# The last token group of a LoRA layer: the weighting and the sum of terms on VectorE by halves, the last products by halves, a store for each tile

## The chip, the cores and the metric

The kernel runs on one NeuronCore of one Trainium2 chip. The metric is the device time of one execution in microseconds (us); lower is better. The time before is 794.3 us, the median of three runs (794.25 to 794.47). The engines are named as in the profile: PE is TensorE (PEld its weight loads), DVE is VectorE, ACT is ScalarE, POOL is GpSimd and SP is SyncE, which here only issues transfers.

## What is computed

The reference is two transformer layers over 2048 tokens of width 256: a long convolution in place of attention, a mixture of 16 experts, a second attention, and last a feed-forward layer with LoRA experts. The change lies in that last layer alone:

```
h = layernorm(x);  logits = h @ Wg.T;  the best K = 2 of 8 experts e, with weights rw
for k in 0, 1:                                  # the two picks of each token
    x1 = h @ W1.T + lora(A1[e_k], B1[e_k])      # F = 896 hidden columns, rank 32
    x3 = h @ W3.T + lora(A3[e_k], B3[e_k])
    x2 = silu(x1) * x3
    out += (x2 @ W2.T + lora(A2[e_k], B2[e_k]) of x2) * rw_k
x = x + out
```

## The kernel before

The last phase (`tail_phase`) works on 8 groups of 256 tokens (`NG` = 8 groups of `TG` = 2 tiles of 128). Of each group the 896 hidden columns are taken in 7 chunks of 128 (`FB` = 7), so that there are 56 chunks F. Each engine runs its own program: a loop over steps S in which chunk S is begun and chunks S-1 and S-2 are finished. The order on an engine is the order of the code, and engines wait for each other by semaphores, each counted up by one kind of instruction. No scheduler moves anything.

For chunk F and pick k, PE forms x1 and x3 (`base` L1442, `low_rank` L1457), ACT applies silu (`silu` L1625), and DVE multiplies by x3 (`product` L1953). All of the two picks' output has the factor of the first pick taken out, so the second pick is weighted by the ratio of the two: POOL multiplies it by `ratio_sb` (`weight` L1748) and adds it to the first (`both` L1753). Products of fp32 values are made as three products of a high and a low part, so ACT copies the high parts (`hidden_high` L1631, L1635) and DVE subtracts to get the low parts (`hidden_low` L1959). Then PE multiplies the hidden columns by A2 (`terms` L1489, 6 products of 512 columns, 3 for each half of the 256 expert ranks, in two PSUM banks) and by W2 (`down` L1502, 6 products of 256 columns).

After its 7th chunk a group is closed. DVE multiplies each half of the terms by the picks' masks (`masked_terms` L1969), POOL sums the two picks (`terms_sum` L1764), ACT and DVE form the high and the low part (`terms_high` L1648, `terms_low` L1975), PE multiplies by B2 (`low_rank_out` L1515, 12 products of 256 columns), DVE adds the group to x (`add_out` L1982) and SP stores its two tiles (`store` L1403). In the groups 0 to 6 this happens while the next group's chunks run. Behind group 7 there is no next one: the whole chain lies open. `LAST_CHUNK` is 56.

Of the kernel before, what the change touches and what calls it, by code (L numbers as in the profile page):

```python
# [1283 lines left out]
TG = 2  # L1284
# [31 lines left out]
def tail_phase(nc, memory, a, stage, slots_dram, out_rows, ident, x_sb, comb_idx, norm, w_hi, w_lo, ctx_ring, banks):  # L1316
# [38 lines left out]
    with ExitStack() as s:  # L1355
# [36 lines left out]
        def _(sp):  # L1392
# [8 lines left out]
            def store(g):  # L1401
                sp.wait_ge(out_added, TG * (g + 1))
                sp.dma_start(out_rows[:, TG * g:TG * g + TG, :], x_sb[:, TG * g:TG * g + TG, :]).then_inc(stored, 16)  # L1403

# [6 lines left out]
            for S in range(FIRST_STEP, END_STEP):  # L1411
# [8 lines left out]
                if n == 3 and 1 <= g <= NG:  # L1420
                    store(g - 1)
            sp.wait_ge(stored, 16 * NG)

        @block.tensor
        def _(pe):
# [53 lines left out]
            def terms(F):  # L1479
# [5 lines left out]
                for half in range(HALVES):  # L1485
                    if n == 0 and g >= 1:
                        pe.wait_ge(t_mul, HALVES * (g - 1) + half + 1)
                    for j, (wp, hp) in enumerate(split_products(weight_cols(n, 5, half), hid)):
                        last = nc.tensor.matmul(term_banks[half][:, :], wp, hp, start=(n == 0 and j == 0),  # L1489
                                                stop=(n == FB - 1 and j == 2))  # L1490
                last.then_inc(terms_done, 1)

# [14 lines left out]
            def low_rank_out(g):  # L1507
                pe.wait_ge(t_lo_done, g + 1)
                for t in range(TG):
                    for half in range(HALVES):  # L1510
                        rows = slice(t * P, (t + 1) * P)
                        cols = slice(4 * DIM + half * DIM, 4 * DIM + (half + 1) * DIM)
                        w = w_hi[:, FB, cols], w_lo[:, FB, cols]
                        for k, (hp, wp) in enumerate(split_products((t_hi[:, half, rows], t_lo[:, half, rows]), w)):
                            last = nc.tensor.matmul(out_banks[g % 2][:, t * DIM:(t + 1) * DIM], hp, wp, start=False,  # L1515
                                                    stop=(half == 1 and k == 2), skip_group_check=True)
                last.then_inc(out_done, 1)
# [96 lines left out]
        def _(act):  # L1614
# [12 lines left out]
            def hidden_high(F):  # L1627
                act.wait_ge(weighted, F + 1)
                if F >= 2:
                    act.wait_ge(terms_done, F - 1)  # L1630
                nc.scalar.copy(hid_hi[:, F % 2, SECOND, :], f[:, F % 2, 1, :]).then_inc(hi_done, 1)  # L1631
# [12 lines left out]
            def terms_high(g):  # L1644
                act.wait_ge(t_sum, g + 1)
                if g >= 1:
                    act.wait_ge(out_done, g)
                nc.scalar.copy(t_hi[:, :, :], mix[:, :, 0:GT]).then_inc(t_hi_done, 1)  # L1648

# [72 lines left out]
        def _(pool):  # L1722
# [62 lines left out]
            for S in range(FIRST_STEP, END_STEP):  # L1785
# [5 lines left out]
                if n == 0 and 0 <= g < NG:  # L1791
                    inputs_low(g, 0)
                if n == 2 and 1 <= g <= NG:
                    terms_sum(g - 1)
# [4 lines left out]
                gathers(S)  # L1799
                if is_chunk(S - 1):  # L1800
                    weight(S - 1)
# [5 lines left out]
        def _(dve):  # L1807
# [143 lines left out]
            def product(F, k):  # L1951
                dve.wait_ge(silu_done, 2 * F + k + 1)
                nc.vector.tensor_tensor(f[:, F % 2, k, :], f[:, F % 2, k, :], x_banks[F % 2][:, GT:2 * GT], ALU.mult)\  # L1953
                  .then_inc(prod_done, 1)

            def hidden_low(F):
                for i, which in enumerate((SECOND, BOTH)):
# [4 lines left out]
            def masked_terms(g):  # L1962
                dve.wait_ge(am_lo_pool, 2 * min(g + 2, NG))
                dve.wait_ge(am_lo_dve, 2 * min(g + 2, NG))
                dve.wait_ge(terms_done, FB * (g + 1))
                for half in range(HALVES):
                    by_kind = [v.rearrange("p (w t) -> p w t", w=PICKS) for v in (mix[:, half, :],
                                                                                 term_banks[half][:, :])]
                    nc.vector.tensor_tensor(by_kind[0], by_kind[1],  # L1969
                                            masks_sb[:, g % 2, :, half * GT:(half + 1) * GT], ALU.mult)\  # L1970
                      .then_inc(t_mul, 1)

            def terms_low(g):
                dve.wait_ge(t_hi_done, g + 1)
                nc.vector.tensor_tensor(t_lo[:, :, :], mix[:, :, 0:GT], t_hi[:, :, :].bitcast(FP32), ALU.subtract)\  # L1975
                  .then_inc(t_lo_done, 1)

# [21 lines left out]
            for S in range(FIRST_STEP, END_STEP):  # L1999
# [25 lines left out]
                if is_chunk(S - 1):  # L2025
                    product(S - 1, 1)
                if of_group:
                    inputs_product(g, 3)
# [94 lines left out]
```

## Time and profile before

| | |
|---|---|
| median of 3 runs | 794.3 us (794.25 to 794.47) |
| the profiled execution | 791.16 us, of which the span is 789.4 us |
| mean granted PE clock | 0.959 of full speed |
| busy share of the span | PE 90%, PEld 81%, DVE 64%, POOL 49%, ACT 43% |

The span runs from the first to the last instruction of the profiled execution; 1.76 us of its time lie around it. All times of rows count from the start of the span. "Idle before" in square brackets is how long the engine had nothing to do, and whose work ended that.

### The profile page before, as it was taken

Reading aid. Unit: us, or ns where it says so; the run is one execution under the profiler, and the core shown is the slowest. Engines: PE = TensorE matmul, PEld = TensorE weight load, DVE = VectorE, ACT = ScalarE, POOL = GpSimd, SP = SyncE. Lnnn points to the kernel's source line nnn. Section 1 sums busy time; section 2 is a strip of 40 time slices with the busy share of each in tenths; the row PEclk is TensorE's granted clock in tenths of the full one; section 3 lists DMA queues with packets and bytes.
Section 4 is the critical chain, followed back from the end, with each engine's and each line's share of the span. In section 5 each row is a group of like instructions: output and inputs, shape, how many; then the busy total and the mean of one; then the engine's idle time right before and its main releaser. Section 6 shows DMA issues by size and latency. Waiting matters only on the chain.

```text
span 789.4 us, 13948 instructions
## 1 busy us (share of the span) xinstructions
PE 713.2 (90%) x4849; PEld 635.7 (81%) x4849; DVE 507.8 (64%) x1296; ACT 340.5 (43%) x698; POOL 384.9 (49%) x450
## 2 busy tenths in 40 slices
PE   4899988959999991778999999999999999999995
PEld 2444557848999980668899999999999999999995
DVE  3999997975666645676566566575574675653422
ACT  2563633245666652265444253444434533443221
POOL 5876956047766605544264363543652643322322
PEclk9999998988999995679999999999999999999999
DMA  8675505946866764424021020010020110000000
GB/s 246 196 166 133 142 27 125 210 108 179 245 195 197 163 146 126 155 71 130 1 61 34 8 61 28 14 59 22 29 63 5 41 41 1 2 15 1 14 1 14
DMA packets 44595, 68.61 MB, mean 87 GB/s; under 512 B 7376, under 2 KB 32240, under 8 KB 44528
## 3 DMA queue, kind: packets, MB, share of 16 engines
q0 software_dynamic: 10080, 28.72, 16.5%
q1 hardware_dynamic: 34352, 38.97, 15.5%
q8 instruction: 41, 0.67, 0.4%
q14 instruction: 26, 0.21, 0.1%
q10 hardware_dynamic: 96, 0.04, 0.0%
HBM read 50.77 MB, written 14.84 MB: 83 GB/s over the span
## 4 chain that ended last, share of the span: by engine, by line
PE 53%; POOL 3%; DVE 2%; ACT 2%; issue 2%; POOLq 0%; DVEq 0%
PE psum L1457 20%; PE psum L1442 10%; PE psum L1489 9%; PE psum L1502 4%; PE psum L1475 3%; PE psum L1538 2%; PE psum L1515 2%; PE psum L1528 2%; POOL rows_back L1728 1%; PE psum L1556 1%; ACT lora_w_hi L1618 1%; DVE lora_w_lo L1819 0%; PE psum L1546 0%; PE psum L1569 0%; PE psum L1576 0%
## 5 line engine op out<-in xcount | busy, mean ns | idle before, releaser
L1953 DVE TENSOR_TENSOR hid<-hid,psum 128x256 f32<-128x256 f32 x112 | 47.0, 420 | 152.2 <-ACT hid L1625 152.2
L1457 PE MATMUL psum<-am_hi,lora_w_hi 128*128 128x256 f32 x448 | 127.4, 284 | 2.0 <-DVE am_lo L1948 2.0
L1748 POOL TENSOR_TENSOR hid<-hid,ratio_sb 128x256 f32<-128x256 f32 x56 | 41.5, 741 | 176.9 <-DVE hid L1953 176.7
L1457 PE MATMUL psum<-am_hi,lora_w_lo 128*128 128x256 f32 x448 | 127.4, 284 | 0.0
L1457 PE MATMUL psum<-am_lo,lora_w_hi 128*128 128x256 f32 x448 | 127.2, 284 | 0.0
L1625 ACT ACTIVATE hid<-psum 128x256 f32<-128x256 f32 x112 | 42.9, 384 | 183.3 <-PE psum L1457 183.2
L1033 POOL DMA_INDIRECT rows_in<-y_scratch,slot_token x80 | 76.0, 950 | 30.9 <-issue 26.5
L1457 PEld LDWEIGHTS psum<-am_hi,lora_w_hi 128*128 128x128 f32 x448 | 86.2, 192 | 2.2 <-POOL am_lo L1759 2.1
L1457 PEld LDWEIGHTS psum<-am_hi,lora_w_lo 128*128 128x128 f32 x448 | 86.3, 193 | 0.0
L1457 PEld LDWEIGHTS psum<-am_lo,lora_w_hi 128*128 128x128 f32 x448 | 86.2, 192 | 0.0
L1728 POOL DMA_INDIRECT rows_back<-slots_scratch,comb_idx x64 | 66.8, 1043 | 39.2 <-POOLq L697 23.7
L1442 PE MATMUL psum<-lora_x_hi,lora_w_hi 128*128 128x256 f32 x224 | 67.8, 302 | 3.5 <-DVE lora_w_lo L1819 3.5
L1959 DVE TENSOR_TENSOR hid_lo<-hid,hid_hi 128x256 fp32r<-128x256 f32 x112 | 56.8, 528 | 13.1 <-ACT hid_hi L1631 8.0
L1442 PE MATMUL psum<-lora_x_lo,lora_w_hi 128*128 128x256 f32 x224 | 63.1, 282 | 0.0
L327 POOL TENSOR_TENSOR kv<-ctx_t 128x1024 f32<-128x1024 f32 (+2 forms) x48 | 57.4, 1284 | 11.6 <-PE psum L448 11.6
L1442 PE MATMUL psum<-lora_x_hi,lora_w_lo 128*128 128x256 f32 x224 | 62.9, 281 | 0.0
L873 PE MATMUL psum<-moe_w_hi,moe_xt_hi 128*128 x160 | 49.2, 307 | 0.0
L591 DVE TENSOR_TENSOR prod<-psum,q_t 128x1024 f32<-128x1024 f32 (+1 forms) x64 | 41.2, 685 | 8.4 <-PE psum L448 6.2
L1442 PEld LDWEIGHTS psum<-lora_x_hi,lora_w_hi 128*128 128x128 f32 x224 | 42.7, 191 | 4.6 <-DVE lora_w_lo L1819 4.2
L873 PE MATMUL psum<-moe_w_lo,moe_xt_hi 128*128 x160 | 45.9, 287 | 0.0
L1489 PE MATMUL psum<-hid_hi,lora_w_hi 128*128 128x512 f32 x112 | 44.6, 398 | 1.3 <-DVE hid_lo L1959 1.3
L873 PE MATMUL psum<-moe_w_hi,moe_xt_lo 128*128 x160 | 45.4, 284 | 0.0
(250 smaller groups left out, 2050.2 us busy)
## 6 DMA issues: line engine op xcount, KB each, us to landing
slots_scratch<-y_out SPq DMA_DIRECT2D x40, 256.0 KB, 3.3
stage<-in_moe_weights SPq DMA_DIRECT2D x18, 384.0 KB, 3.8
moe_w_lo<-in_moe_weights POOLq DMA_DIRECT2D x18, 384.0 KB, 7.1
lora_stage_early<-in_lora_weights SPq DMA_DIRECT2D x16, 384.0 KB, 3.5
x_sb<-in_x SPq DMA_DIRECT2D x4, 512.0 KB, 6.3
ctx_t<-in_ctx_t SPq DMA_DIRECT2D x4, 512.0 KB, 7.3
y_scratch<-y SPq DMA_DIRECT2D x8, 256.0 KB, 2.2
x_sb<-shared_out POOLq DMA_DIRECT2D x4, 512.0 KB, 5.3
```

The costliest lines, as they stand in the source:

```text
L327: last = nc.gpsimd.tensor_tensor(kv[:, n % KV_SLOTS, :, first:first + shape[2] * shape[3]].rearrange("p n (i j) -> p n i j", j=shape[3]), ...
L591: last = nc.vector.tensor_tensor(prod[:, :, j, i], y_ji, query[:, :, i].unsqueeze(2).broadcast_to(shape), ALU.mult)
L873: last = nc.tensor.matmul(gu_banks[q % 2][:, k * DIM:(k + 1) * DIM], xp, wp, start=(c == 0 and j == 0), stop=(c == HALVES - 1 and j == 2))
L1033: nc.gpsimd.indirect_dma_start(out=rows_in[:, i % ROW_SLOTS, :], out_offset=None, in_=y_dram[:, :], in_offset=bass.IndirectOffsetOnAxis(ap ...
L1442: nc.tensor.matmul(x_banks[F % 2][:, w * GT:(w + 1) * GT], wp, xp, start=(w == 0 and c == 0 and k == 0), stop=False, skip_group_check=True)
L1457: last = nc.tensor.matmul(x_banks[F % 2][:, w * GT:(w + 1) * GT], wp, ap, start=False, stop=(half == 1 and k == 2), skip_group_check=True)
L1489: last = nc.tensor.matmul(term_banks[half][:, :], wp, hp, start=(n == 0 and j == 0), stop=(n == FB - 1 and j == 2))
L1625: nc.scalar.activation(f[:, F % 2, k, :], x_banks[F % 2][:, 0:GT], ACT.Silu).then_inc(silu_done, 1)
L1728: nc.gpsimd.indirect_dma_start(out=rows_back[:, t % ROW_TILES, k * DIM:(k + 1) * DIM], out_offset=None, in_=slots_dram[:, :], in_offset=ba ...
L1748: nc.gpsimd.tensor_tensor(f[:, F % 2, 1, :], f[:, F % 2, 1, :], ratio_sb[:, F // FB % 2, :], ALU.mult)\
L1953: nc.vector.tensor_tensor(f[:, F % 2, k, :], f[:, F % 2, k, :], x_banks[F % 2][:, GT:2 * GT], ALU.mult)\
L1959: nc.vector.tensor_tensor(hid_lo[:, F % 2, which, :], f[:, F % 2, which, :], hid_hi[:, F % 2, which, :].bitcast(FP32), ALU.subtract).then_ ...
```

## The change

It touches what follows the last chunk of group 7, and the form of a few semaphores elsewhere.

1. The last chunk (F = 55) is weighted and summed by DVE (`weight_last`), no longer by POOL.
2. `terms_done` counts each half of the terms; in group 7 DVE starts on half 0 with the first count, and sums the two picks itself, half by half.
3. High and low parts of group 7's terms are made by halves of 256 columns in place of 512 at once.
4. `low_rank_out` takes the halves of the ranks in its outer loop and the tiles in the inner one (in all groups), and in group 7 waits for each half on its own.
5. Group 7's two tiles are stored by two transfers of 128 KB in place of one of 256 KB, each behind its own addition.

```diff
--- before.py
+++ after.py
@@ -1399,8 +1399,10 @@
                 load_ctx(sp, a, ctx_ring, b, ctx_loaded[b % CTX_SLOTS])
 
             def store(g):
-                sp.wait_ge(out_added, TG * (g + 1))
-                sp.dma_start(out_rows[:, TG * g:TG * g + TG, :], x_sb[:, TG * g:TG * g + TG, :]).then_inc(stored, 16)
+                step = TG if g < NG - 1 else 1
+                for t in range(TG * g, TG * g + TG, step):
+                    sp.wait_ge(out_added, t + step)
+                    sp.dma_start(out_rows[:, t:t + step, :], x_sb[:, t:t + step, :]).then_inc(stored, 16)
 
             sp.dma_start(gate_sb[:, :, :], a["lora_gate"]).then_inc(gate_loaded, 16)
             for t in range(TG):
@@ -1419,7 +1421,7 @@
                             load_context(t + CTX_SLOTS)
                 if n == 3 and 1 <= g <= NG:
                     store(g - 1)
-            sp.wait_ge(stored, 16 * NG)
+            sp.wait_ge(stored, 16 * (NG - 1 + TG))
 
         @block.tensor
         def _(pe):
@@ -1488,7 +1490,7 @@
                     for j, (wp, hp) in enumerate(split_products(weight_cols(n, 5, half), hid)):
                         last = nc.tensor.matmul(term_banks[half][:, :], wp, hp, start=(n == 0 and j == 0),
                                                 stop=(n == FB - 1 and j == 2))
-                last.then_inc(terms_done, 1)
+                    last.then_inc(terms_done, 1)
 
             def down(F):
                 g, n = F // FB, F % FB
@@ -1506,8 +1508,10 @@
 
             def low_rank_out(g):
                 pe.wait_ge(t_lo_done, g + 1)
-                for t in range(TG):
-                    for half in range(HALVES):
+                for half in range(HALVES):
+                    if half == 1 and g == NG - 1:
+                        pe.wait_ge(t_lo_done, NG + 1)
+                    for t in range(TG):
                         rows = slice(t * P, (t + 1) * P)
                         cols = slice(4 * DIM + half * DIM, 4 * DIM + (half + 1) * DIM)
                         w = w_hi[:, FB, cols], w_lo[:, FB, cols]
@@ -1627,7 +1631,7 @@
             def hidden_high(F):
                 act.wait_ge(weighted, F + 1)
                 if F >= 2:
-                    act.wait_ge(terms_done, F - 1)
+                    act.wait_ge(terms_done, HALVES * (F - 1))
                 nc.scalar.copy(hid_hi[:, F % 2, SECOND, :], f[:, F % 2, 1, :]).then_inc(hi_done, 1)
                 act.wait_ge(both_done, F + 1)
                 if F >= 2:
@@ -1642,10 +1646,15 @@
                 nc.scalar.copy(am_hi[:, kind, w, :], mix[:, w, :]).then_inc(am_hi_done, 1)
 
             def terms_high(g):
-                act.wait_ge(t_sum, g + 1)
                 if g >= 1:
                     act.wait_ge(out_done, g)
-                nc.scalar.copy(t_hi[:, :, :], mix[:, :, 0:GT]).then_inc(t_hi_done, 1)
+                if g < NG - 1:
+                    act.wait_ge(t_sum, g + 1)
+                    nc.scalar.copy(t_hi[:, :, :], mix[:, :, 0:GT]).then_inc(t_hi_done, 1)
+                    return
+                for half in range(HALVES):
+                    act.wait_ge(t_sum, g + half + 1)
+                    nc.scalar.copy(t_hi[:, half, :], mix[:, half, 0:GT]).then_inc(t_hi_done, 1)
 
             def exponentials(G):
                 for k in range(TG):
@@ -1790,14 +1799,14 @@
                         attention_rstd(first, first + (1 if G == 0 else TG))
                 if n == 0 and 0 <= g < NG:
                     inputs_low(g, 0)
-                if n == 2 and 1 <= g <= NG:
+                if n == 2 and 1 <= g < NG:
                     terms_sum(g - 1)
                 if n == 2 and G is not None:
                     router_rstd(G)
                 if n == 3 and G is not None:
                     x_low_part(G)
                 gathers(S)
-                if is_chunk(S - 1):
+                if is_chunk(S - 1) and S < LAST_CHUNK:
                     weight(S - 1)
                     both(S - 1)
                 if n == 0 and 0 <= g < NG:
@@ -1953,6 +1962,15 @@
                 nc.vector.tensor_tensor(f[:, F % 2, k, :], f[:, F % 2, k, :], x_banks[F % 2][:, GT:2 * GT], ALU.mult)\
                   .then_inc(prod_done, 1)
 
+            def weight_last(F):
+                dve.wait_ge(ratio_copied, F // FB + 1)
+                dve.wait_ge(prod_done, 2 * F + 2)
+                nc.vector.tensor_tensor(f[:, F % 2, 1, :], f[:, F % 2, 1, :], ratio_sb[:, F // FB % 2, :], ALU.mult)\
+                  .then_inc(weighted, 1)
+                dve.wait_ge(weighted, F + 1)
+                nc.vector.tensor_tensor(f[:, F % 2, 0, :], f[:, F % 2, 0, :], f[:, F % 2, 1, :], ALU.add)\
+                  .then_inc(both_done, 1)
+
             def hidden_low(F):
                 for i, which in enumerate((SECOND, BOTH)):
                     dve.wait_ge(hi_done, 2 * F + i + 1)
@@ -1962,18 +1980,31 @@
             def masked_terms(g):
                 dve.wait_ge(am_lo_pool, 2 * min(g + 2, NG))
                 dve.wait_ge(am_lo_dve, 2 * min(g + 2, NG))
-                dve.wait_ge(terms_done, FB * (g + 1))
+                if g < NG - 1:
+                    dve.wait_ge(terms_done, HALVES * FB * (g + 1))
                 for half in range(HALVES):
+                    if g == NG - 1:
+                        dve.wait_ge(terms_done, HALVES * FB * NG - HALVES + half + 1)
                     by_kind = [v.rearrange("p (w t) -> p w t", w=PICKS) for v in (mix[:, half, :],
                                                                                  term_banks[half][:, :])]
                     nc.vector.tensor_tensor(by_kind[0], by_kind[1],
                                             masks_sb[:, g % 2, :, half * GT:(half + 1) * GT], ALU.mult)\
                       .then_inc(t_mul, 1)
+                    if g == NG - 1:
+                        dve.wait_ge(t_mul, HALVES * g + half + 1)
+                        nc.vector.tensor_tensor(mix[:, half, 0:GT], mix[:, half, 0:GT], mix[:, half, GT:2 * GT], ALU.add)\
+                          .then_inc(t_sum, 1)
 
             def terms_low(g):
-                dve.wait_ge(t_hi_done, g + 1)
-                nc.vector.tensor_tensor(t_lo[:, :, :], mix[:, :, 0:GT], t_hi[:, :, :].bitcast(FP32), ALU.subtract)\
-                  .then_inc(t_lo_done, 1)
+                if g < NG - 1:
+                    dve.wait_ge(t_hi_done, g + 1)
+                    nc.vector.tensor_tensor(t_lo[:, :, :], mix[:, :, 0:GT], t_hi[:, :, :].bitcast(FP32), ALU.subtract)\
+                      .then_inc(t_lo_done, 1)
+                    return
+                for half in range(HALVES):
+                    dve.wait_ge(t_hi_done, g + half + 1)
+                    nc.vector.tensor_tensor(t_lo[:, half, :], mix[:, half, 0:GT], t_hi[:, half, :].bitcast(FP32),
+                                            ALU.subtract).then_inc(t_lo_done, 1)
 
             def add_out(g):
                 dve.wait_ge(out_done, g + 1)
@@ -2024,6 +2055,8 @@
                     router_masks(G)
                 if is_chunk(S - 1):
                     product(S - 1, 1)
+                if S == LAST_CHUNK:
+                    weight_last(S - 1)
                 if of_group:
                     inputs_product(g, 3)
                 if n == 1:
```

On DVE, this is what follows the product of the last chunk, first before and then after. `hid` is the hidden chunk, `mix` holds the masked terms, `t_hi` and `t_lo` their high and low parts, and x_sb the residual stream.

```order
L1953 TENSOR_TENSOR hid<-hid,psum 128x256 [waits silu_done]
L1959 TENSOR_TENSOR hid_lo<-hid,hid_hi 128x256 [waits hi_done] x2
L1969 TENSOR_TENSOR mix<-psum,masks_sb 128x512 [waits terms_done,am_lo_dve,am_lo_pool]
L1969 TENSOR_TENSOR mix<-psum,masks_sb 128x512
L1975 TENSOR_TENSOR t_lo<-mix,t_hi 128x512 [waits t_hi_done]
L1982 SCALAR_TENSOR_TENSOR x_sb<-psum,lora_first_w,x_sb 128x256 [waits first_w_done,out_done]
L1982 SCALAR_TENSOR_TENSOR x_sb<-psum,lora_first_w,x_sb 128x256
```

```order
L1962 TENSOR_TENSOR hid<-hid,psum 128x256 [waits silu_done]
L1968 TENSOR_TENSOR hid<-hid,ratio_sb 128x256 [waits prod_done,ratio_copied]
L1971 TENSOR_TENSOR hid<-hid 128x256 [waits weighted]
L1977 TENSOR_TENSOR hid_lo<-hid,hid_hi 128x256 [waits hi_done] x2
L1990 TENSOR_TENSOR mix<-psum,masks_sb 128x512 [waits terms_done,am_lo_dve,am_lo_pool]
L1995 TENSOR_TENSOR mix<-mix 128x256 [waits t_mul]
L1990 TENSOR_TENSOR mix<-psum,masks_sb 128x512 [waits terms_done]
L1995 TENSOR_TENSOR mix<-mix 128x256 [waits t_mul]
L2006 TENSOR_TENSOR t_lo<-mix,t_hi 128x256 [waits t_hi_done] x2
L2013 SCALAR_TENSOR_TENSOR x_sb<-psum,lora_first_w,x_sb 128x256 [waits first_w_done,out_done]
L2013 SCALAR_TENSOR_TENSOR x_sb<-psum,lora_first_w,x_sb 128x256
```

Two instructions on `hid` stand ahead of the low parts, two sums on `mix` stand between and behind the masked products, and the low part `t_lo` is made in two.

On SP, this is the end of the list of transfers, before and then after. The rows on `ctx_ring` load a tile of the context for the second attention; `x4` and `x3` stand for so many stores in a row.

```order
L1403 DMA out_x<-x_sb 128x2x256 [waits out_added]
L1276 DMA ctx_ring<-in_ctx_keys 128x256 [waits scaled_done]
L1277 DMA ctx_ring<-in_ctx_t 128x2x128
L1403 DMA out_x<-x_sb 128x2x256 [waits out_added] x4
L1355 UNCONDITIONAL_BRANCH [waits stored]
```

```order
L1405 DMA out_x<-x_sb 128x2x256 [waits out_added]
L1276 DMA ctx_ring<-in_ctx_keys 128x256 [waits scaled_done]
L1277 DMA ctx_ring<-in_ctx_t 128x2x128
L1405 DMA out_x<-x_sb 128x2x256 [waits out_added] x3
L1405 DMA out_x<-x_sb 128x256 [waits out_added] x2
L1355 UNCONDITIONAL_BRANCH [waits stored]
```

The last of the four stores of two tiles has become two stores of one tile each.

On POOL, `weight` and `both` of chunk 55 and the last `terms_sum` are gone; its program ends with chunk 54. On PE no product is added or taken away: the last 12 are the same, with their order by halves, and the seventh has a wait of its own for `t_lo`. On ACT the last copy of 512 columns has become two of 256.

## Rows read from the trace of the kernel before

**Rows 1.** The head of the page

```profile
span 789.4 us, 13948 instructions
```

**Rows 2.** Timeline, the last chunk (start us, us, engine, line, operation, out<-in)

```profile
774.24 0.42 DVE L1953 TENSOR_TENSOR hid<-hid,psum 128x256 f32<-128x256 f32 x1 [2.03 <-ACT hid L1625]
...
774.74 0.73 POOL L1748 TENSOR_TENSOR hid<-hid,ratio_sb 128x256 f32<-128x256 f32 x1 [3.43 <-DVE hid L1953]
...
775.56 0.73 POOL L1753 TENSOR_TENSOR hid<-hid 128x256 f32<-128x256 f32 x1
...
776.32 0.40 ACT L1635 CAST hid_hi<-hid 128x256 fp32r<-128x256 f32 x1 [0.40 <-POOL hid L1753]
...
776.75 0.43 DVE L1959 TENSOR_TENSOR hid_lo<-hid,hid_hi 128x256 fp32r<-128x256 f32 x1 [0.19 <-ACT hid_hi L1635]
...
777.24 0.50 PE L1489 MATMUL psum<-hid_hi,lora_w_hi 128*128 128x512 f32 x1 [1.33 <-DVE hid_lo L1959]
```

**Rows 3.** Timeline, the last terms, their masks, sum and parts

```profile
777.80 0.40 PE L1489 MATMUL psum<-hid_hi,lora_w_lo 128*128 128x512 f32 x1
...
778.51 0.39 PE L1489 MATMUL psum<-hid_hi,lora_w_lo 128*128 128x512 f32 x1
...
778.74 0.28 PE L1502 MATMUL psum<-lora_w_hi,hid_hi 128*128 128x256 f32 x1
...
779.04 1.29 DVE L1969 TENSOR_TENSOR mix<-psum,masks_sb 128x512 f32<-128x512 f32 x2 [1.85 <-PE psum L1489]
...
779.33 0.28 PE L1502 MATMUL psum<-lora_w_hi,hid_lo 128*128 128x256 f32 x1
...
780.40 1.26 POOL L1764 TENSOR_TENSOR mix<-mix 128x512 f32<-128x512 f32 x1 [4.12 <-DVE mix L1969]
...
781.70 0.62 ACT L1648 CAST t_hi<-mix 128x512 fp32r<-128x512 f32 x1 [4.97 <-POOL mix L1764]
...
782.35 0.69 DVE L1975 TENSOR_TENSOR t_lo<-mix,t_hi 128x512 fp32r<-128x512 f32 x1 [2.02 <-ACT t_hi L1648]
```

**Rows 4.** Timeline, the last products, addition and store

```profile
783.09 0.58 PE L1515 MATMUL psum<-lora_w_hi,t_hi 128*128 128x256 f32 x1 [3.49 <-DVE t_lo L1975]
...
786.06 0.88 DVE L1982 SCALAR_TENSOR_TENSOR x_sb<-psum,lora_first_w,x_sb 128x256 f32<-128x256 f32 x2 [3.02 <-PE psum L1515]
...
786.96 0.37 SPq L1403 DMA_DIRECT2D out_x<-x_sb  x1
```

**Rows 5.** Windows, granted clock third from the end, around the last products

```profile
782.50:782.75 0.25, 0.00 (x0) 0.00 (x0) 0.25 (x1) 0.00 (x0) 0.00 (x0) 0.81 0.00 0
...
783.25:784.00 0.75, 0.75 (x4) 0.75 (x5) 0.00 (x0) 0.00 (x0) 0.00 (x0) 0.50 0.00 0
```

**Rows 6.** Timeline, the same products and addition in group 0

```profile
419.10 0.39 PE L1515 MATMUL psum<-lora_w_hi,t_hi 128*128 128x256 f32 x1
...
420.82 0.48 DVE L1982 SCALAR_TENSOR_TENSOR x_sb<-psum,lora_first_w,x_sb 128x256 f32<-128x256 f32 x1 [0.47 <-PE psum L1515]
```

**Rows 7.** Timeline, three other starts of PE after a wait

```profile
379.13 0.39 PE L1442 MATMUL psum<-lora_x_hi,lora_w_hi 128*128 128x256 f32 x1 [1.25 <-DVE lora_w_lo L1819]
...
110.51 2.82 PE L461 MATMUL psum<-ident,q_t 128*128 128x128 f32 x12 [2.24 <-DVE q_t L598]
...
122.84 0.63 PE L473 MATMUL psum<-ident,y 128*128 128x128 f32 x4 [1.41 <-ACT moe_x_t L375]
```

**Rows 8.** Windows, the clock before the first and after the third of those

```profile
378.00:379.00 1.00, 0.00 (x0) 0.00 (x0) 0.89 (x2) 0.81 (x2) 0.00 (x0) 1.00 0.00 0
...
123.50:124.00 0.50, 0.50 (x6) 0.50 (x5) 0.38 (x1) 0.49 (x1) 0.00 (x0) 0.88 0.82 283
```

**Rows 9.** Transfers (bytes each, median us from issue to landing)

```profile
out_x<-x_sb SPq DMA_DIRECT2D x8, 256.0 KB, 2.1
...
shared_down_w<-in_moe_weights SPq DMA_DIRECT2D x2, 128.0 KB, 2.1
```

**Rows 10.** Windows, transfer rate of the last store (last column GB/s)

```profile
788.20:788.40 0.20, 0.00 (x0) 0.00 (x0) 0.00 (x0) 0.00 (x0) 0.00 (x0) 1.00 1.09 389
```

## Prediction

> **What bounds the kernel now.** I read the page first: a span of 789.4 us [rows 1], with PE busy for 90% of it. Anything that the change does while the groups overlap must pass through PE; anything behind the last chunk is open, since no other work is left. So I went from the page to the timeline of the last 16 us, instruction by instruction, and asked of each which one released it.
>
> The reader is to see one thread that runs through all engines, with one of them working at a time. The last product on DVE begins at 774.24. POOL weights it from 774.74 and sums from 775.56, 0.73 each; ACT copies the high part at 776.32, DVE subtracts at 776.75, and PE, idle for 1.33, starts the terms at 777.24 [rows 2]. The third product of half 0 starts at 777.80, that of half 1 at 778.51, DVE masks both halves from 779.04 (1.29), POOL sums from 780.40 (1.26), ACT copies from 781.70 (0.62), DVE subtracts from 782.35 (0.69) [rows 3]. PE, idle for 3.49, starts the last products at 783.09, DVE adds from 786.06 (0.88), SP issues the store at 786.96 [rows 4], and it lands 2.1 later [rows 9]. Each step begins within 0.1 of the end of the one ahead of it, but for DVE at 779.04, which is 0.53 behind the start of the last terms product; I keep that 0.53.
>
> The clock is the second thing to see. PE ended its last `down` at 779.61 (779.33 + 0.28) [rows 3]. While it waited the granted clock fell, within 782.50 to 782.75 (mean 0.81), and stood at 0.50, the 1.2 GHz level, through the last products [rows 5]. So from the first product to the addition it took 2.97 (783.09 to 786.06) [rows 4]; the same 12 products at full clock, in group 0, took 1.72 (419.10 to 420.82) [rows 6]. This is 1.25 us that the last wait costs on top of itself.
>
> **The change part by part.** I carry the same thread forward with durations from these rows. Between engines I take the gap that the rows show, 0.03 between DVE and ACT (776.32 + 0.40 to 776.75) and 0.06 from DVE to PE (777.18 to 777.24) [rows 2]; a wait of DVE on its own result shows in none of them, and I take 0.03 too, bounded by 0 and by the 0.08 from DVE to POOL (774.66 to 774.74) [rows 2].
>
> *Weighting on DVE.* A DVE operation on 128x256 values took 0.43 with POOL idle [rows 2]. From the end of the product, 774.66: two of them with gaps, to 775.58; ACT 775.61 to 776.01; DVE 776.04 to 776.47; PE at 776.53. That is 0.71 earlier. The copy and the subtraction of the second pick fit in between (ready at 775.12, needed by 776.04), since ACT is free. Behind `weight_last` on DVE stand only the two low parts that wait for it in any case, so its wait holds up nobody. POOL loses its last two instructions and nobody waits for them.
>
> *Masks and sums by halves.* All moves up by 0.71. Half 0 is released 0.53 behind 777.80 - 0.71, at 777.62: mask 0.65 to 778.27, sum to 778.73. Half 1 was ready at 778.33 and waits for DVE: mask 778.76 to 779.41, sum 779.44 to 779.87. ACT made the high part of half 0 meanwhile; the low part of half 0 stands behind the second sum in DVE's order and runs 779.90 to 780.33. ACT's copy of half 1 runs 779.90 to 780.30, DVE's low part 780.36 to 780.79. PE starts at 780.39. It was 783.09, so 2.70 is gained up to here, 0.71 of it before and 1.99 in this part. DVE is now the engine that is late: six operations in a row, 2.7 us of them.
>
> A page speaks against this part. By the Trainium skill, "VectorE: DVE Perf Modes", section "The TRN2 errata — SBUF-src ops pay a fixed extra latency per instruction", each Vector instruction pays a fixed amount, and pieces of 512 elements or more are advised; its formula for fp32 tensor_tensor, (N + 151) / 0.96, gives an estimated 424 ns for 256 columns and 691 ns for 512. The trace agrees (0.43 and 0.69), so a split low part costs 0.86 of DVE in place of 0.69. By that rule alone the halves would lose 0.17; the sum here stays as it is, because only one half lies ahead of PE's start.
>
> *Last products.* The same twelve. The first six take 0.8 at full clock (half of 1.72), so the seventh is wanted at 781.2, and the second low part is there by 780.8: its new wait is passed at once. The order half by half costs nothing, since each product loads its own weights in either order. Now PE's idle time runs from 778.90 (779.61 - 0.71) to 780.39, 1.5 us in place of 3.49. Which clock it finds is the large unknown. Full clock gives 1.72 and gains 1.25; the low one gives 2.97 and gains nothing. For full clock: PE came back from 1.25 of idle time at 379.13 [rows 7] with the clock at 1.00 throughout the gap [rows 8], and from 1.33 at 777.24 [rows 2] with no change to be seen in its products (777.80 to 778.51, 0.24 each [rows 3]). Against it: after 2.24 idle at 110.51, and, worse, after 1.41 at 122.84 [rows 7] the clock fell within 123.50 to 124.00 (mean 0.88) though PE was at work [rows 8]. Ahead of that one PE had been on small transposes and 16-column products; here it comes from full 512- and 256-column ones. I take full clock.
>
> *Stores.* The second tile's store is issued behind its own addition, the last one, as the single store was; the first goes out 0.44 earlier and, at 0.37 to issue [rows 4], is out of SP's way. 256 KB at 389 GB/s [rows 10] is 0.67 of the 2.1, so half the bytes save at most 0.33; the nearest 128 KB transfers, two loads in a row, also took 2.1 [rows 9], which saves nothing. I take 0.2. By the Trainium skill, "DMA: Bandwidth & Descriptors", section "Anatomy of one DMA — SWDGE (gpsimd) path", a transfer costs about 2.0 us fixed and its bytes at 436 GB/s: an estimated saving of 0.3 (that path is GpSimd's, this one SP's, so no run here shows it).
>
> *What is spread over all groups.* `terms_done` is counted up 56 times more. The product that counts it, at 778.51, is followed by the next at 778.74 [rows 3], 0.23, the same pitch as the others: no cost. In groups 0 to 6 the waits are met by the same event as before, and `low_rank_out` has other order and equal work.
>
> The sum: 0.71 + 1.99 + 1.25 + 0.2 = 4.15. The profiled execution took 791.16 with 1.76 around the span; its own sum is 787.0. The median of the runs is 3.1 above that execution, a difference that has nothing to do with the end, so the median goes from 794.3 to about 790.1. Within 0.2% (1.6 us) a measurement of this kernel can't tell a change from none.
>
> **The rivals.**
> *The clock falls anyway* (15%). The gap of 1.5 is longer than the 1.25 and 1.33 that left it alone and longer than the 1.41 after which it fell. Then the last products take 2.97, or something between where it falls midway: 790.1 to 791.4.
> *The two stores get in each other's way* (6%). If the second can't begin until the first has landed, it waits for 2.1 - 0.44 = 1.7 and then takes its own time: 790.1 + 0.2 + 1.7 = 792.0, or less where only its bytes wait. Against it: the two 128 KB loads, issued in a row, both took 2.1 [rows 9].
> *The halves don't overlap* (6%), so that the change doesn't do what it says: PE starts only when both low parts are there, 780.85, or DVE's waits on itself are long. At 0.08 a wait the six of them cost 0.3. It gives 790.4 to 790.9, hardly to be told from the forecast by time, but by the timeline.
> *The counted products stall PE* (3%), the one that ends slower. The place is the third product of half 0 in each of 56 chunks. It costs 56 times its price, and PE is never idle there, so all of it shows. It eats the gain at 4.15 / 56 = 0.07 us each, and decides for slower by 0.2% at (4.15 + 1.6) / 56 = 0.10. The 0.23 pitch speaks against any price at all.
> *The end isn't what counts* (4%): something outside the profiled thread, in runs without the profiler, hides most of the gain; 793 or more. No row speaks for it.
>
> **How the numbers follow.** The forecast, 789.6 to 790.5 at full clock, has 66%. Together with the clock's, the stores' and the halves' cases, all faster, it makes 93%. The end case gives same (4%), the counted products slower (3%). The range goes from 789.3 (a store that saves 0.33 and waits of DVE at 0 and with starts that overlap the end ahead of them, 0.7 in all) to 791.4, where the low clock costs its full 1.25; the stores' case, the end case and the slower one lie above it, 13% together.
>
> **What would show it.** In the new profile: DVE's two operations right behind the last product and the first of the last terms some 2.3 behind the start of that product, where it was 3.0; two masks with a sum behind each; PE's last idle time near 1.5 with 1.00 beside it; twelve products and the wait for them in 1.7; two stores 0.44 apart, the second landing 1.8 to 2.1 behind its issue. The prediction is wrong if the last products run at 0.50, if the seventh waits, or if PE's rows in the groups before are longer than 0.28.

## The result, and the profile after

The changed kernel takes 789.24 us (median of 6 runs, 788.13 to 789.82). The kernel before took 793.81 us in the same comparison (6 runs, 793.14 to 794.47). The ratio is 0.9942, with an interval of 0.9929 to 0.9954: 4.6 us less, between 3.7 and 5.6. The forecast was 790.1 us and 4.15 us less, with a range of 789.3 to 791.4; the measured time lies 0.06 us below it.

The profiled execution took 789.12 us. Its span, from the head of its page:

```profile
span 787.4 us, 13953 instructions
```

That is only 2.0 us less than the 789.4 of before [rows 1], so the first thing to look at is where the two differ. The last product on DVE starts at 776.50, where it was 774.24 [rows 2]: everything up to there, which the change doesn't touch, took 2.26 us longer in this execution. From that product to the end of the span it is 787.4 - 776.50 = 10.90 us, against 789.4 - 774.24 = 15.16 before. I call this stretch **the end**; it is 4.26 us shorter. The timeline of the end after the change, instruction by instruction, answers to [rows 2 to 4]:

```profile
776.50 0.42 DVE L1962 TENSOR_TENSOR hid<-hid,psum 128x256 f32<-128x256 f32 x1 [2.04 <-ACT hid L1629]
...
777.03 0.42 DVE L1968 TENSOR_TENSOR hid<-hid,ratio_sb 128x256 f32<-128x256 f32 x1
...
777.49 0.42 DVE L1971 TENSOR_TENSOR hid<-hid 128x256 f32<-128x256 f32 x1
...
777.93 0.88 DVE L1977 TENSOR_TENSOR hid_lo<-hid,hid_hi 128x256 fp32r<-128x256 f32 x2
...
778.86 0.50 PE L1491 MATMUL psum<-hid_hi,lora_w_hi 128*128 128x512 f32 x1 [0.70 <-DVE hid_lo L1977]
...
779.43 0.40 PE L1491 MATMUL psum<-hid_hi,lora_w_lo 128*128 128x512 f32 x1
...
779.97 0.69 DVE L1990 TENSOR_TENSOR mix<-psum,masks_sb 128x512 f32<-128x512 f32 x1 [1.16 <-PE psum L1491]
...
780.69 0.42 DVE L1995 TENSOR_TENSOR mix<-mix 128x256 f32<-128x256 f32 x1
...
781.04 0.68 DVE L1990 TENSOR_TENSOR mix<-psum,masks_sb 128x512 f32<-128x512 f32 x1
...
781.75 0.43 DVE L1995 TENSOR_TENSOR mix<-mix 128x256 f32<-128x256 f32 x1
782.10 0.98 DVE L2006 TENSOR_TENSOR t_lo<-mix,t_hi 128x256 fp32r<-128x256 f32 x2
782.21 0.41 ACT L1657 CAST t_hi<-mix 128x256 fp32r<-128x256 f32 x1 [0.60 <-DVE mix L1995]
...
782.57 0.39 PE L1519 MATMUL psum<-lora_w_hi,t_hi 128*128 128x256 f32 x1 [1.33 <-DVE t_lo L2006]
...
783.38 0.28 PE L1519 MATMUL psum<-lora_w_hi,t_hi 128*128 128x256 f32 x1
...
784.28 0.87 DVE L2013 SCALAR_TENSOR_TENSOR x_sb<-psum,lora_first_w,x_sb 128x256 f32<-128x256 f32 x2 [1.21 <-PE psum L1519]
784.79 0.82 SPq L1405 DMA_DIRECT2D out_x<-x_sb  x2
```

Read it against the steps. The weighting: product at 776.50, first terms product on PE at 778.86, 2.36 in place of 3.00. Masks, sums and parts: 778.86 to 782.57, 3.71 in place of 5.85. The last products and the wait for them: 782.57 to 784.28, 1.71 in place of 2.97. Additions, store and landing: 784.28 to 787.4, 3.12 in place of 3.34. The seventh last product, 783.38, follows at the same pitch as the others: its wait is passed at once, though the second low part ends only at 783.08. The windows of the same execution (granted clock third from the end, GB/s last) answer to [rows 5, 10]:

```profile
782.20:782.50 0.30, 0.00 (x0) 0.00 (x0) 0.30 (x1) 0.29 (x1) 0.00 (x0) 1.00 0.00 0
782.57:784.00 1.43, 1.43 (x12) 1.43 (x12) 0.42 (x1) 0.05 (x1) 0.00 (x0) 1.00 0.00 0
...
785.80:786.00 0.20, 0.00 (x0) 0.00 (x0) 0.00 (x0) 0.00 (x0) 0.00 (x0) 1.00 1.02 358
786.00:786.20 0.20, 0.00 (x0) 0.00 (x0) 0.00 (x0) 0.00 (x0) 0.00 (x0) 1.00 0.38 128
786.20:786.40 0.20, 0.00 (x0) 0.00 (x0) 0.00 (x0) 0.00 (x0) 0.00 (x0) 1.00 1.02 364
```

The clock is at 1.00 ahead of the last products and through them. The two stores show as two bursts with a dip between. Their landing, from the view of the storing line in the last stretch, answers to [rows 9]:

```profile
L1405 SPq DMA_DIRECT2D out_x<-x_sb x2: 345/387/429, 784.8 to 785.2; - x2
...
DMA to landing us min/median/max: 1.7/1.7/1.8
```

Each of the two lands 1.7 to 1.8 behind its issue, where the one of 256 KB took 2.1.

### The profile page after: what moved, and what is told of

The parts are those of the page before. It is cut to its first block, busy times and chain, and to the rows that moved or that the text cites. A ratio compares the mean times of both kernels' runs of the same rounds, so it can differ in the third digit from the quotient of the medians.

```text
span 787.4 us, 13953 instructions
## 1 busy us (share of the span) xinstructions
PE 713.0 (91%) x4849; PEld 636.5 (81%) x4849; DVE 509.1 (65%) x1301; ACT 340.5 (43%) x699; POOL 382.7 (49%) x447
## 4 chain that ended last, share of the span: by engine, by line
PE 53%; DVE 3%; POOL 2%; ACT 2%; issue 1%; DVEq 0%; POOLq 0%
PE psum L1459 20%; PE psum L1444 10%; PE psum L1491 9%; PE psum L1504 4%; PE psum L1477 3%; PE psum L1542 2%; PE psum L1519 2%; PE psum L1532 2%; POOL rows_back L1737 1%; PE psum L1560 1%; ACT lora_w_hi L1622 1%; DVE lora_w_lo L1828 0%; PE psum L1550 0%; PE psum L1573 0%; PE psum L1580 0%
```

## The experiments

Times of single executions lie far apart, so each experiment is read by its end (start of the last product on DVE to the end of the span), beside the ratio where there is one. "Before" has an end of 15.16 and the changed kernel one of 10.90.

| kernel | span | end | ratio to before, interval |
|---|---|---|---|
| only what is in all groups | 815.6 | 15.21 | 1.0006, 0.9986 to 1.0025 |
| only the weighting | 816.8 | 14.34 | 0.9995, 0.9978 to 1.0013 |
| only the halves | 810.9 | 11.76 | 0.9967, 0.9945 to 0.9988 |
| only the stores | 789.0 | 14.89 | |
| the changed kernel | 811.4 | 10.90 | 0.9948, 0.9932 to 0.9963 |
| the changed kernel, again | 787.1 | 10.88 | 0.9938, 0.9916 to 0.9960 |
| before, PE kept at work | 791.1 | 13.90 | 0.9992, 0.9973 to 1.0011 |
| changed, PE kept at work | 783.3 | 10.85 | |
| changed, a bank for the last tile | 788.3 | 10.47 | 0.9930, 0.9905 to 0.9955 |
| the same, again | 786.3 | 10.48 | 0.9943, 0.9924 to 0.9962 |
| changed, PE waits longer by one operation | 788.1 | 11.51 | |
| changed, PE waits longer by two | 787.8 | 12.34 | |

**What is spread over all groups, alone.** The kernel before with these edits (those on PE are shown; the waits of ACT and DVE on `terms_done` are set to the doubled count):

```diff
-                last.then_inc(terms_done, 1)
+                    last.then_inc(terms_done, 1)
...
-                for t in range(TG):
-                    for half in range(HALVES):
+                for half in range(HALVES):
+                    for t in range(TG):
```

> The kernel before with only what the change does in all groups: terms_done counted for each half (56 more counts on PE) and low_rank_out with the halves outside the tiles. The end of the last group is as before. The end means here from the start of the last product on DVE to the end of the span: 15.2 us before, 10.9 after. My theory, all of the gain lies in the end: time equal to before within 0.2% (1.6 us), the end 15.2. Rival 1, the gain beyond the 4.26 that the two ends show comes from these spread edits: 0.3 to 1.3 us faster. Rival 2, the counts cost PE: slower by 56 times their price, 0.07 us each would be 4 us.

817.38 us against 817.3 (29 runs), an end of 15.21. No effect is seen, within 1.1 us less and 2.0 us more. The rival that ends slower falls: at 0.10 us a count the ratio would be 1.007, and at 0.07 it would still be 1.005. A gain of some tenths from these edits, which the first rival of the expectation allows, is not excluded.

**The weighting, alone.** `weight_last` in place of `weight` and `both` for chunk 55.

> The kernel before with only the weighting and summing of the last chunk on DVE. Theory: product start to first terms product 2.36 in place of 3.00 us, all behind it as before with the clock at 0.50 in the last products, the end 14.5 us (15.2 - 0.64). Time 0.6 us less, within what a measurement can tell. Rival, the slack is taken up by the next wait: the end stays 15.2.

Its timeline (last product on DVE, first terms product, first of the last products):

```profile
802.46 0.42 DVE L1953 TENSOR_TENSOR hid<-hid,psum 128x256 f32<-128x256 f32 x1 [2.03 <-ACT hid L1625]
...
804.82 0.50 PE L1489 MATMUL psum<-hid_hi,lora_w_hi 128*128 128x512 f32 x1 [0.70 <-DVE hid_lo L1968]
...
810.67 0.39 PE L1515 MATMUL psum<-lora_w_hi,t_hi 128*128 128x256 f32 x1 [3.48 <-DVE t_lo L1984]
```

802.46 to 804.82 is 2.36, as in the changed kernel: 0.64 is gained and the next wait doesn't take it up (3.48, as before). The end is 14.34, though, 0.18 less than expected, and the reason is the clock. Its windows around the last products:

```profile
810.67:811.00 0.33, 0.33 (x2) 0.33 (x3) 0.00 (x0) 0.00 (x0) 0.00 (x0) 0.94 0.00 0
811.00:813.40 2.40, 2.39 (x12) 2.10 (x10) 0.00 (x0) 0.00 (x0) 0.00 (x0) 0.50 0.00 0
```

PE had waited 3.48, came back with the clock still high, and the clock fell about 0.3 us later; DVE's additions started at 813.43, so the products and the wait for them took 2.76. What the low clock costs thus differs between executions with the same wait: 2.97 in three profiled ones (before, only the spread edits, only the stores) and 2.76 here, where full clock takes 1.71.

**The halves, alone.** The changed kernel with the weighting and the store of before.

> The changed kernel with the last chunk weighted by POOL as before and the last store in one piece: halves of terms, sums on DVE, parts and products by halves are left. Theory: first terms product to first last product 3.71 in place of 5.85 us, the 12 products and the wait for them 1.71 in place of 2.97, the end 15.2 - 2.14 - 1.26 = 11.8 us; time 3.4 us less than before. Rival, the clock falls because PE still waits 1.3 us here and its earlier wait is 1.33 and not 0.70: the products at 2.97, the end 13.0, time 2.1 us less.

The timeline of its first terms product, first last product and additions:

```profile
802.13 0.50 PE L1489 MATMUL psum<-hid_hi,lora_w_hi 128*128 128x512 f32 x1 [1.33 <-DVE hid_lo L1975]
...
805.84 0.39 PE L1517 MATMUL psum<-lora_w_hi,t_hi 128*128 128x256 f32 x1 [1.33 <-DVE t_lo L2004]
...
807.55 0.88 DVE L2011 SCALAR_TENSOR_TENSOR x_sb<-psum,lora_first_w,x_sb 128x256 f32<-128x256 f32 x2 [1.21 <-PE psum L1517]
```

First terms product to first last product 3.71, products and wait 1.71, end 11.76: the first theory, to 0.04. With the earlier wait back at 1.33 and the last one at 1.33 as well, the clock stayed. This version holds both the move of the sums from POOL to DVE and the work by halves, and no run takes the two apart. By the rows, 0.69 of the 2.14 is DVE's earlier start: its first mask begins 1.11 behind the first terms product (778.86 to 779.97 in the changed kernel), where it began 1.80 behind (777.24 to 779.04). An estimate for the move of the sum alone is 0.6: a DVE operation on 512 columns took 0.69 and POOL's sum 1.26.

**The stores, alone.**

> The kernel before with only the last group's store in two pieces of one tile, each behind its own addition. Theory: from the start of the additions to the end of the span 3.1 us in place of 3.3, because 128 KB land 1.7 behind their issue and not 2.1; the end 15.0 in place of 15.2. Rival, the two transfers hinder each other: the second lands 2.1 or more behind its issue and the end stays 15.2 or grows.

From the additions to the end of the span 3.08 in place of 3.34, the two landing at 1.7 and 1.8. The end is 14.89. The rival falls: issued about 0.45 behind the first, the second landed no more than 0.1 later behind its issue than the first did.

**The changed kernel beside the one before, once more.**

> The changed kernel itself, once more, beside the kernel before on the same chip and in the same rounds. Theory, the gain is the 4.26 us of the end and the forecast missed by the level of the kernel before, which lay 0.5 us lower in the later runs than in the runs shown: 3.9 to 4.6 us less than before. Rival, a part of the gain lies outside the end: more than 4.8 us less.

812.95 us against 817.3, a ratio of 0.9948, which is 4.3 us (3.0 to 5.6). The level of all kernels was 24 us higher in this set of comparisons: the first attention product (`att_y` with `ctx_ring`) starts at 335.7 where the changed kernel had 312.5, and from there to the end of the span it is 475.7 and 474.9. The end was 10.90 again.

**PE kept at work in its wait.** Products of 256 columns that nobody reads, into a free PSUM bank, ahead of the last `low_rank_out`:

```diff
+            def keep_busy(count):
+                for _ in range(count):
+                    nc.tensor.matmul(att_banks[1][:, 0:GT], w_hi[:, 0, 0:P], x_hi[:, 1, 0, :], start=True, stop=True)
...
+                if S == LAST_CHUNK + 2:
+                    keep_busy(26)
                 if n == 2 and 1 <= g <= NG:
                     low_rank_out(g - 1)
```

In the kernel before, 26 of them:

> The kernel before with 26 products that nobody reads (256 columns, into a free bank) on PE between the last down and the last products, some 3.1 us of the 3.49 in which it waits. Nothing else differs. Theory, the clock falls because PE is idle: it stays at 1.00, the 12 products and the wait for them take 1.7 in place of 2.97, the end 13.9 in place of 15.2, time 1.3 us less. Rival, the clock isn't what makes them slow, or the extra products delay the first real one: the end 15.2 or more.

Its timeline (last product on DVE, first last product, additions), and the window of the products with the clock third from the end:

```profile
777.20 0.42 DVE L1959 TENSOR_TENSOR hid<-hid,psum 128x256 f32<-128x256 f32 x1 [2.03 <-ACT hid L1631]
...
786.08 0.38 PE L1515 MATMUL psum<-lora_w_hi,t_hi 128*128 128x256 f32 x1 [0.47 <-DVE t_lo L1981]
...
787.79 0.88 DVE L1988 SCALAR_TENSOR_TENSOR x_sb<-psum,lora_first_w,x_sb 128x256 f32<-128x256 f32 x2 [1.77 <-PE psum L1515]
```

```profile
786.08:787.00 0.92, 0.92 (x7) 0.92 (x8) 0.00 (x0) 0.00 (x0) 0.00 (x0) 1.00 0.00 0
```

The end is 13.90, 1.26 less, all of it between 786.08 and 787.79: 1.71 at a clock of 1.00. The real products wait only for `t_lo`, as before, and their start lies 8.88 behind DVE's last product, where it was 8.85. This shows the cause of the 1.25 in the profile: with PE at work through the wait the clock stays. It is one execution, against four with PE idle in which the clock fell, three times ahead of the products and once (the weighting alone) just behind their start. The times don't resolve it (0.9992, 0.9973 to 1.0011; 1.26 us would be 0.9984).

In the changed kernel, 9:

> The changed kernel with 9 such products in PE's last wait, some 1.1 of 1.33 us. Theory: the clock is at 1.00 without them too, so nothing changes: the end 10.9. Rival, a wait of 1.33 costs clock in some executions: here never, and the end stays 10.9 at best, with the first products at the low level in other runs of the changed kernel.

The end is 10.85: nothing is left to gain. Its span of 783.3 is the shortest of all and shows what a single time is worth: its last product on DVE started at 772.45, 4 us ahead of the 776.50 above, though all the work up to there is the same.

**How near the changed kernel is to losing the clock.** One or two more DVE operations ahead of the low parts, on a buffer that is no longer used:

```diff
+                for i in range(1):
+                    nc.vector.tensor_tensor(rows_back[:, 0, 2 * DIM * i:2 * DIM * (i + 1)], rows_back[:, 1, 0:2 * DIM],
+                                            rows_back[:, 1, 2 * DIM:4 * DIM], ALU.add)
                 for half in range(HALVES):
                     dve.wait_ge(t_hi_done, g + half + 1)
```

> The changed kernel with one more DVE operation of 512 columns (0.69 us, result unused) ahead of the last low parts, so that PE waits 2.0 us in place of 1.33 before the last products. Theory, a wait of some 2 us is still short enough: the clock at 1.00, the products in 1.71, the end 10.9 + 0.7 = 11.6. Rival, the changed kernel is just short of the fall: the clock at 0.50 in the products, the end up to 12.8.

The timeline of its first last product, and the window of the products:

```profile
783.26 0.39 PE L1519 MATMUL psum<-lora_w_hi,t_hi 128*128 128x256 f32 x1 [1.93 <-DVE t_lo L2009]
```

```profile
783.26:784.90 1.64, 1.64 (x12) 1.47 (x12) 0.28 (x1) 0.00 (x0) 0.00 (x0) 1.00 0.00 0
```

PE waited 1.93, the products and the wait for them took 1.72 and the clock stayed at 1.00: an end of 11.51.

And with two:

> As the one before with two such operations: PE waits 2.7 us. Theory: between the wait that keeps the clock (1.33) and the one that loses it (3.49) there is no fixed point to be had from one execution, since it fell after 1.41 and after 2.24 in the kernel before; here I expect it to fall, within the products or ahead of them: the end 12.3 at full clock, up to 13.5 at the low one. Rival: it stays at 1.00 and the end is 12.3.

The timeline of its first last product and additions, and the windows around them:

```profile
782.73 0.39 PE L1519 MATMUL psum<-lora_w_hi,t_hi 128*128 128x256 f32 x1 [2.54 <-DVE t_lo L2009]
...
784.73 0.88 DVE L2016 SCALAR_TENSOR_TENSOR x_sb<-psum,lora_first_w,x_sb 128x256 f32<-128x256 f32 x2 [1.72 <-PE psum L1519]
```

```profile
783.00:783.50 0.50, 0.50 (x6) 0.50 (x6) 0.01 (x1) 0.00 (x0) 0.00 (x0) 1.00 0.00 0
783.50:784.00 0.50, 0.50 (x6) 0.50 (x5) 0.00 (x0) 0.00 (x0) 0.00 (x0) 0.94 0.00 0
784.00:784.70 0.70, 0.69 (x4) 0.40 (x2) 0.00 (x0) 0.00 (x0) 0.00 (x0) 0.50 0.00 0
```

PE waited 2.54 (from 780.19 to 782.73), came back at 1.00, and the clock fell within 783.50 to 784.00 while it worked, as it had after 1.41 in [rows 7, 8]; the products and the wait for them took 2.00. The end of 12.34 is the number of the rival, a clock that stays, but for another reason: the wait grew by 1.21 and not by the 1.4 expected, and the fall put 0.28 on top. Only the windows tell the two apart. One execution each: the changed kernel kept the clock in all its 3 profiled executions, and a wait of 1.93 kept it once. How often it falls at such waits isn't settled.

**A version that ends sooner.** In the changed kernel DVE adds both tiles behind the last product, because they share a PSUM bank. Here tile 1 of the last group has a bank of its own:

```diff
+                        bank = att_banks[0] if g == NG - 1 and t == 1 else out_banks[g % 2]
...
-                last.then_inc(out_done, 1)
+                        if half == 1 and (t == TG - 1 or g == NG - 1):
+                            last.then_inc(out_done, 1)
```

> The changed kernel, in which tile 1 of the last group is summed in a PSUM bank of its own (a bank of the attention, free by then), so that DVE adds tile 0 while PE makes the last three products of tile 1. Theory: the two additions no longer stand behind the last product together; DVE starts 0.35 earlier (three products at 0.12) and ends 0.35 to 0.4 earlier, the end 10.5 in place of 10.9. Rival, the stores set the end: the second store waits for the first's issue (0.37 to 0.43) and the end is 10.8.

The timeline of the first last product, the additions and the stores:

```profile
783.90 0.39 PE L1524 MATMUL psum<-lora_w_hi,t_hi 128*128 128x256 f32 x1 [1.33 <-DVE t_lo L2012]
...
785.26 0.88 DVE L2023 SCALAR_TENSOR_TENSOR x_sb<-psum,lora_first_w,x_sb 128x256 f32<-128x256 f32 x2 [0.86 <-PE psum L1524]
...
785.77 0.82 SPq L1405 DMA_DIRECT2D out_x<-x_sb  x2
```

The additions start 1.36 behind the first product in place of 1.71, and the end is 10.47, 0.43 less than in the changed kernel. Its ratio, 0.9930, looked like more than that, so both were timed again together:

> The changed kernel beside the kernel before once more, after runs in which single executions of one kernel lay up to 7 us apart. Theory, the gain is what the last group's end shows, 4.26 us: the median of the ratios near 0.9946, the end 10.9 us in the profiled execution whatever its span. Rival, something ahead of the end gains too: a ratio below 0.9935, and marks such as the first product of the attention (312 us) earlier than in the kernel before by more than executions differ.

> The version with a bank of its own for the last tile, once more beside the changed kernel. Theory: the end 10.5 us, 0.43 less than the changed kernel's, too little for the times to tell: both ratios within each other's intervals. Rival, its first ratio (0.993) was more than the end's 4.7 us because the other bank helps elsewhere: its ratio stays 0.15% below that of the changed kernel.

0.9938 (0.9916 to 0.9960) for the changed kernel and 0.9943 (0.9924 to 0.9962) for this one: times can't tell them apart, the ends can (10.88 and 10.48). The first attention product came at 312.7 in the changed kernel's profile, where the kernel before had 311.2, so no row speaks for a gain ahead of the end. The version with its own bank is the best here, by 0.4 us in the profile alone.

## Why the prediction was right and where it failed

**The thread and its terms.** The mechanism held: weighting 0.71 forecast, 0.64 measured; masks, sums and parts 1.99 and 2.14; last products 1.25 and 1.26; store 0.2 and 0.22; together 4.15 and 4.26. That the sum is off by only 0.11 is in part luck, since 0.07 too much and 0.15 too little partly cancel, and the store's 0.2 was a choice between 0 and 0.33. The weighting is 0.07 short because DVE starts it 0.11 behind the product's end (776.92 to 777.03), not 0.03: this instruction waits for two counts, `prod_done` and `ratio_copied`, and the next one, with one wait, starts 0.04 behind. That the second wait is the cause was not tried alone. That the operation ahead reads PSUM is not the cause, since the masked product reads it too and its sum starts 0.03 behind (780.66 to 780.69). The halves gain 0.15 more mainly because an operation that doesn't need the one ahead starts some 0.07 before that one's end (781.04 against 781.11; 782.10 against 782.18), where the sum had put 0.03 behind it. The same overlap hid in the 1.29 of the two masks before, so half of it, 0.65, was too short for one: they took 0.69 and 0.68. DVE became the late engine of this stretch, as forecast: it works from 779.97 until PE starts at 782.57, with no gap above 0.03.

**The clock.** The likeliest case held: PE's last wait was 1.33, not the 1.5 of the sum, and the clock stayed. The rows could not decide this beforehand, and the prediction gave the low clock 15%; that it came out so is in part luck, though a wait of 1.93 kept the clock too in the one execution tried. That the gain comes from the wait and not from the split was shown by keeping PE at work in the kernel before.

**The rivals.** Stores that hinder each other, counted products that stall PE, halves that don't overlap and an end that doesn't count all fell, the first two in experiments of their own. The prediction's sign for the stall, longer rows of PE, didn't come either: the products of `down` take 280 to 282 ns on average, 279 to 281 before. The ends add up too: 0.82 for the weighting (0.64 without its luck with the clock), 3.40 for the halves, 0.27 for the stores, 4.31 with the 0.64, against 4.26.

**What failed: the level and the range around it.** The step is "the median goes from 794.3 to about 790.1", and with it "The range goes from 789.3": the level of the kernel before, 794.3, the median of three runs 0.22 us apart, went in as if it were exact, and the range took in only the bounds of the terms. The prediction itself had the figure that was missing, "Within 0.2% (1.6 us)", and put none of it into the range. The runs showed 793.81 in place of 794.3 with three more runs, so 0.49 of the miss of 0.91 (790.15 less 789.24) is this level; 0.11 is the terms, and the other 0.31 stays open, inside the interval of 3.7 to 5.6 around the 4.6.

Executions of one kernel differ far more than those three did: the 17 runs of before beside the stores' experiment span 789.41 to 796.59, and the three profiled executions of the changed kernel have spans of 787.4, 811.4 and 787.1 around ends of 10.90, 10.90 and 10.88. The profiled execution shows it too: the prediction's own sum for it was 787.0, it took 789.12, and the stretch ahead of the last product alone took 2.26 us more than in the execution that the sum started from. An allowance of about 1 us on either side, the half width of that interval, would have put the low end at 788.3 and held the result.

The comparisons of the changed kernel (4.6, 4.3 and 4.9 us less) all hold 4.26; a further gain of some tenths outside the end can't be excluded, and nothing points to it.

## What to carry to other kernels

Behind the last piece of work every wait lies open: follow the one thread through the engines, move short steps to the engine that already has the data, and halve what is left so that the next engine starts on the first half. Count the second price of PE's wait too: where its clock fell during or just behind the wait of 3.5 us here, the next 12 products cost 1.05 to 1.26 us more. Read an edit of some us in a program of 800 by a stretch of the profile that it alone touches, and give the total a range that holds the uncertainty of the level it starts from, and not only that of its terms.

## What the runs showed of the hardware

The last stores, from SP, landed in 1.7 to 1.8 with 128 KB and in 2.1 with 256 KB, in all profiled executions. The granted clock could fall after PE had come back: 0.3 us into the products after a wait of 3.48, and about 1.2 after one of 2.54. And the same program had a level of 793 us in some comparisons and of 817 in others, one chip at both levels in turn; 23 of the extra 24 us lie in the routed experts' stage: PE's last group of products ahead of it starts at 165.95 at either level, the last product of the stage at 319.2 in place of 296.1. Why was not looked into.
